# Integer softmax of an attention layer: row sums and three of eight value diagonals on GpSimd, one activation table set for logarithm and exponential

## The reference, cut to what matters

```python
x_int = x / scaling_factor
x_int = x_int - x_int.max(axis=-1, keepdims=True)
x0_int = jnp.floor(x0 / scaling_factor)
x_int = jnp.maximum(x_int, n * x0_int)
q = jnp.floor(x_int / x0_int)
r = x_int - x0_int * q
...
z = r * (r + b_int) + c_int
exp_int = jnp.maximum(jnp.floor(z * 2.0 ** (n - q)), 0.0)
exp_sum = exp_int.sum(axis=-1, keepdims=True)
ratio = jnp.round(exp_sum / jnp.maximum(exp_int, 1.0))
...
rounds = _log_round(ratio)
...
return jnp.where(mask, 0.0, 2.0 ** (-qlog))
```

## Time and profile before

| | |
|---|---|
| time, median of 3 runs | 598.61 us (598.5 to 599.84) |
| the profiled execution, span from first to last instruction | 604.2 us |
| busy in the span | PE 495.1, DVE 319.2, ACT 206.6, POOL 154.5 us |
| mean granted PE clock | 0.909 of full speed |
| part of the span that the change touches | about 139 to 187 us |

### The profile page before, as it was taken

How to read it: one execution, slowest core, us unless ns; L and a number is a source line. 1 busy time by engine, 2 the same in 40 slices (tenths; PEclk the granted TensorE clock), 3 DMA queues, 4 the chain that set the end, 5 groups by cost and what they waited for, 6 DMA issues and landing times.

```text
span 604.2 us, 12487 instructions
## 1 busy us (share of the span) xinstructions
PE 495.1 (82%) x4400; PEld 457.5 (76%) x4401; DVE 319.2 (53%) x1037; ACT 206.6 (34%) x441; POOL 154.5 (26%) x148
## 2 busy tenths in 40 slices
PE   4999999986443596799998399767999999999960
PEld 4999996575442485799997286756999999999950
DVE  1668999788999786122221356892222222222207
ACT  3630014868984164233334052260121112121110
POOL 1592000000001002465433000005444543443220
PEclk9999999999567686999999589879999999999995
DMA  8995000000009123587779900022666655667117
GB/s 314 408 335 160 15 1 1 1 3 1 0 2 312 30 105 118 168 210 192 162 234 322 295 4 0 1 106 59 190 190 192 201 164 164 190 182 211 34 49 291
DMA packets 40659, 84.86 MB, mean 140 GB/s; under 512 B 7270, under 2 KB 23186, under 8 KB 39586
## 3 DMA queue, kind: packets, MB, share of 16 engines
q1 hardware_dynamic: 33218, 72.81, 37.0%
q0 software_dynamic: 7392, 11.41, 8.3%
HBM read 70.33 MB, written 13.86 MB: 139 GB/s over the span
## 4 chain that ended last, share of the span: by engine, by line
PE 69%; DVE 16%; DMA 6%; ACT 4%; issue 2%; another core or an unknown queue 1%; POOL 0%; SPq 0%; DVEq 0%; ACTq 0%; POOLq 0%
PE ps L1137 18%; PE ps L887 14%; PE ps L1113 12%; PE ps L1121 6%; DMA made<-xT,to_i 3%; DVE h L1924 2%; PE ps L827 2%; PE ps L1002 1%; PE ps L974 1%; DVE xT L1771 1%; PE ps L975 1%; PE ps L1104 1%; PE ps L867 1%; PE ps L868 1%; PE ps L852 1%
## 5 line engine op out<-in xcount | busy, mean ns | idle before, releaser
L1137 PE MATMUL ps<-arena,xn 128*128 x696 | 123.1, 327 | 2.1 <-ACT xn L777 2.1
L1137 PEld LDWEIGHTS ps<-arena,xn 128*128 128x128 f32 x696 | 111.8, 190 | 4.2 <-issue 4.0
L515 POOL DMA_INDIRECT xT<-rows,from_i x58 | 56.3, 971 | 175.8 <-DVE from_i L1785 127.5
L530 POOL DMA_INDIRECT made<-xT,to_i x58 | 67.8, 1170 | 100.9 <-DVE xT L1823 65.9
L887 PE MATMUL ps<-arena 128*128 128x192 f32 (+1 forms) x588 | 85.6, 336 | 9.0 <-ACT arena L556 9.0
L887 PEld LDWEIGHTS ps<-arena 128*128 128x128 f32 (+1 forms) x588 | 83.9, 196 | 9.3 <-ACT arena L556 8.6
L1113 PE MATMUL ps<-xn,arena 128*128 128x128 f32 x696 | 87.2, 275 | 3.2 <-DVE xn L1813 3.2
L1113 PEld LDWEIGHTS ps<-xn,arena 128*128 128x128 f32 x696 | 84.9, 192 | 3.5 <-issue 3.5
L780 ACT ACTIVATE xn<-ps 128x384 f32<-128x384 f32 x78 | 32.6, 493 | 144.7 <-PE ps L1123 110.0
L1811 DVE COPY xn<-ps 128x128 f32<-128x128 f32 x58 | 16.9, 292 | 118.9 <-PE ps L1105 98.2
L777 ACT ACTIVATE xn<-ps,b_all 128x128 f32<-128x128 f32 x114 | 30.8, 389 | 63.5 <-PE ps L1123 51.9
(11 more groups left out here) (373 smaller groups left out, 765.6 us busy)
## 6 DMA issues: line engine op xcount, KB each, us to landing
arena<-ffn_a SPq DMA_DIRECT2D x58, 384.0 KB
arena<-ffn_b SPq DMA_DIRECT2D x116, 96.0 KB
arena<-x_blocks SPq DMA_DIRECT2D x16, 384.0 KB, 7.0
arena<-x_strips SPq DMA_DIRECT2D x3, 1536.0 KB, 12.2
arena<-ffn SPq DMA_DIRECT2D x4, 1152.0 KB
rows<-xn SPq DMA_DIRECT2D x8, 384.0 KB, 2.3
arena<-made SPq DMA_DIRECT2D x8, 384.0 KB, 6.6
arena<-tok_w SPq DMA_DIRECT2D x8, 288.0 KB, 7.3
```

The costliest lines, as they stand in the source:

```text
L515: pool.indirect_dma_start(sx[:, k % 6], None, F["src"], bass.IndirectOffsetOnAxis(from_i[:, k:k + 1], 0)).then_inc(sem(f"sx_in{k % 6}"), 16)
L530: pool.indirect_dma_start(F["made"], bass.IndirectOffsetOnAxis(to_i[:, k:k + 1], 0), yo[:, k % 3], None, compute_op=(ALU.add, ALU.bypass)[ ...
L1137: mm = pe.matmul(ps[:, result_bank(k, N), 0:DIM], hT[:, u % 2, 128 * c:128 * c + 128], F["w2"][:, bass.ds(e2 + DIM * c, DIM)], start=(c == ...
```

## The change

Four things are done in the softmax:

1. The row sums leave DVE. POOL makes them from `Ee` by adding 8 to 8, 4 to 4, 2 to 2 and 1 to 1 elements of each row, in a buffer `pairs` of its own, and DVE waits for them (`row_sums`) ahead of the last instruction of `ratios`.
2. Since POOL still reads `Ee` then, `ratios` begins in another buffer, `quot`, and comes back to `Ee` with its last instruction. `quot` lies where `wx` lies, so `weights(0)` waits for the second `ratio`.
3. POOL makes three of the eight diagonals: (0, part 0) and (1, part 0) ahead of the row sums, as soon as the first values and the masks are there, and (3, part 1) after them. ACT makes the other five, in another order.
4. ACT loads one table set, `natural_log_exp_and_others`, ahead of its wait for the scalars (L675), for both Ln and Exp.

Beside that, semaphores are merged: `tok_b_in` into `cst_in`, `b2_in` into `ffn_in0`, `ones_row`, `gate_set` and `wnat_set` into `pool_set`, `gate_logit` and `soft_in` into `exp_in`, and `gate_exp` and `soft_exp` into `exp_out`, with the counts that are waited for raised to match.

```diff
+        quot = view(18432, [3072])
...
-            sp.dma_start(tok_b_row[:], tok_b).then_inc(sem("tok_b_in"), 16)
+            sp.dma_start(tok_b_row[:], tok_b).then_inc(sem("cst_in"), 16)
...
-            sp.wait_ge(sem("cst_in"), 16)
+            sp.wait_ge(sem("cst_in"), 32)
...
-            sp.dma_start(b2_all, ffn0_b2.to_broadcast([128, E0 * DIM])).then_inc(sem("b2_in"), 16)
+            sp.dma_start(b2_all, ffn0_b2.to_broadcast([128, E0 * DIM])).then_inc(sem("ffn_in0"), 16)
...
+            def on_diagonal(j, part):
+
+                b = slice(96 * part, 96 * part + 96)
+                v_rows = v_sb.rearrange("p t (h d) -> p (t h) d", h=HEADS)
+                pool.tensor_scalar(vbd[:, b, j, :], v_rows[:, b], stat[:, 244 + j:245 + j], None,
+                                   ALU.mult).then_inc(sem("v_pool"), 1)
+
+            def row_sums(part):
+
+                pool.wait_ge(sem("exp_int"), part + 1)
+                E = Ee[:, 1536 * part:1536 * part + 1536].rearrange("p (a b) -> p a b", b=16)
+                pairs = view(24960, [96, 8])
+                link(pool.tensor_tensor(pairs, E[:, :, 0:8], E[:, :, 8:16], ALU.add))
+                for half in (4, 2):
+                    link(pool.tensor_tensor(pairs[:, :, 0:half], pairs[:, :, 0:half], pairs[:, :, half:2 * half], ALU.add))
+                pool.tensor_tensor(rsum[:, 96 * part:96 * part + 96], pairs[:, :, 0], pairs[:, :, 1], ALU.add
+                                   ).then_inc(sem("row_sums"), 1)
+
+            pool.wait_ge(sem("r_ready"), 1)
+            pool.wait_ge(sem("v_act"), 4)
+            on_diagonal(0, 0)
+            on_diagonal(1, 0)
+            row_sums(0)
+            pool.wait_ge(sem("row_sums"), 1)
+            row_sums(1)
+            pool.wait_ge(sem("v_act"), 8)
+            on_diagonal(3, 1)
             pool.wait_ge(sem("o_ps"), 4)
...
+            act.preload_act_table_set("natural_log_exp_and_others")
             act.wait_ge(sem("scalars"), 1)
...
             guess(1)
+            on_diagonal(2, 0)
             thirds(0)
-            on_diagonal(0, 0)
-            on_diagonal(1, 0)
-            on_diagonal(2, 0)
+            on_diagonal(3, 0)
+            on_diagonal(0, 1)
             thirds(1)
-            on_diagonal(3, 0)
-            for j in range(4):
-                on_diagonal(j, 1)
+            on_diagonal(1, 1)
+            on_diagonal(2, 1)
...
-                pe.wait_ge(sem("v_act"), 12 if tq < 2 else 16)
+                pe.wait_ge(sem("v_act"), 10 if tq < 2 else 13)
+                pe.wait_ge(sem("v_pool"), 2 if tq < 2 else 3)
...
             def exponentials(part):
-                c, b = part_of[part]
+                c = part_of[part][0]
                 dve.wait_ge(sem("power_ready"), 2 * part + 2)
                 dve.scalar_tensor_tensor(Ee[:, c], Ee[:, c], k_sq, half_ps[part], ALU.add, ALU.mult).then_inc(sem("exp_int"), 1)
-                dve.wait_ge(sem("exp_int"), part + 1)
-                link(dve.tensor_reduce(rsum[:, b], rows(Ee[:, c]), AX.X, ALU.add))
 
             def ratios(part):
 
-                R = Ee[:, part_of[part][0]]
+                E, R = Ee[:, part_of[part][0]], quot[:, part_of[part][0]]
                 dve.wait_ge(sem("guess"), part + 1)
-                link(dve.scalar_tensor_tensor(R, R, 2.0 ** -30, half_ps[part], ALU.mult, ALU.mult))
+                link(dve.scalar_tensor_tensor(R, E, 2.0 ** -30, half_ps[part], ALU.mult, ALU.mult))
                 link(dve.scalar_tensor_tensor(R, R, 2.0, half_ps[part], ALU.subtract, ALU.mult))
-                dve.scalar_tensor_tensor(rows(R.bitcast(I32)), rows(R), -2.0 ** -30, across(rsum, part), ALU.mult,
+                dve.wait_ge(sem("row_sums"), part + 1)
+                dve.scalar_tensor_tensor(rows(E.bitcast(I32)), rows(R), -2.0 ** -30, across(rsum, part), ALU.mult,
                                          ALU.mult).then_inc(sem("ratio"), 1)
...
+                if part == 0:
+                    dve.wait_ge(sem("ratio"), 2)
```

More of the change, by code:

```diff
@@ L479, in link @@
                 pool.wait_ge(sem("pool_step"), steps[0])
-            pool.memset(xT1[K1:128, :], 1.0).then_inc(sem("ones_row"), 1)
-            pool.wait_ge(sem("ones_row"), 1)
+            pool.memset(xT1[K1:128, :], 1.0).then_inc(sem("pool_set"), 1)
+            pool.wait_ge(sem("pool_set"), 1)
             link(pool.memset(wnat[96:128, 5:7, :], 0.0))
             for w in gate_w1:
-                pool.memset(w[K1:128], 0.0).then_inc(sem("gate_set"), 1)
-            pool.memset(wnat[64:128, 4, :], 0.0).then_inc(sem("wnat_set"), 1)
-            pool.wait_ge(sem("wnat_set"), 1)
+                pool.memset(w[K1:128], 0.0).then_inc(sem("pool_set"), 1)
+            pool.memset(wnat[64:128, 4, :], 0.0).then_inc(sem("pool_set"), 1)
+            pool.wait_ge(sem("pool_set"), 4)
             pool.wait_ge(sem("w_row"), 1)
@@ L505, in _ @@
                 pool.tensor_tensor(s[:, 0, :], s[:, 0, :], s[:, 2, :], ALU.add).then_inc(sem("w_sums"), 1)
+            def on_diagonal(j, part):
[21 more added lines that the diff above has]
+            on_diagonal(3, 1)
             pool.wait_ge(sem("o_ps"), 4)
-            pool.memset(aqT1[K1:K1 + 3], 1.0).then_inc(sem("ones_row"), 1)
+            pool.memset(aqT1[K1:K1 + 3], 1.0).then_inc(sem("pool_set"), 1)
             def exchange(F):
@@ L810, in _ @@
             ins.then_inc(sem("lin_a"), 1)
-            act.wait_ge(sem("gate_logit"), 1)
-            act.activation(stat[:, 501:502], stat[:, 500:501], ACT.Exp, scale=-1.0).then_inc(sem("gate_exp"), 1)
+            act.wait_ge(sem("exp_in"), 1)
+            act.activation(stat[:, 501:502], stat[:, 500:501], ACT.Exp, scale=-1.0).then_inc(sem("exp_out"), 1)
             transposed(3)
-            act.wait_ge(sem("soft_in"), 1)
+            act.wait_ge(sem("exp_in"), 2)
             d16 = rt[:, 432:448]
-            act.activation(d16, d16, ACT.Exp).then_inc(sem("soft_exp"), 1)
+            act.activation(d16, d16, ACT.Exp).then_inc(sem("exp_out"), 1)
             all_norms(1)
@@ L860, in logits @@
                 if i == 0:
-                    pe.wait_ge(sem("gate_set"), 2)
+                    pe.wait_ge(sem("pool_set"), 3)
                 pe.wait_ge(sem("xT0_ready"), 4 * (1 + 2 * n) + i + 1)
@@ L929, in _ @@
                     if (name, b) == ("m2", 1):
-                        pe.wait_ge(sem("cst_in"), 16)
+                        pe.wait_ge(sem("cst_in"), 32)
                         pe.wait_ge(sem("w_sums"), 2)
-                        pe.wait_ge(sem("tok_b_in"), 16)
                         pe.matmul(ps[:, 4, 0:DIM], ones, sum_g[:, 0, :], start=True, stop=True)
@@ L954, in _ @@
             pe.wait_ge(sem("bias_in"), 16 * BIASES)
-            pe.wait_ge(sem("ones_row"), 1)
+            pe.wait_ge(sem("pool_set"), 1)
             def qk_free(n):
@@ L1062, in _ @@
             pe.wait_ge(sem("aq_act"), 5)
-            pe.wait_ge(sem("ones_row"), 2)
+            pe.wait_ge(sem("pool_set"), 5)
             pe.wait_ge(sem("wp_ready"), 2)
@@ L1173, in experts @@
                 up(1, 1, 0)
-                pe.wait_ge(sem(f"ffn_in{n}"), 16 if n == 0 else 16 * E1 // 2)
+                pe.wait_ge(sem(f"ffn_in{n}"), 32 if n == 0 else 16 * E1 // 2)
                 pe.wait_ge(sem(f"tiles_ready{n}"), 1)
@@ L1348, in _ @@
             dve.wait_ge(sem("blk_read"), 16)
-            dve.wait_ge(sem("cst_in"), 16)
+            dve.wait_ge(sem("cst_in"), 32)
             away, away_sq = stat[:, 100:101], stat[:, 101:102]
@@ L1464, in _ @@
             token_row(1)
-            dve.wait_ge(sem("wnat_set"), 1)
+            dve.wait_ge(sem("pool_set"), 4)
             dve.wait_ge(sem("wnat_in"), 128)
@@ L1736, in route @@
                     link(dve.tensor_tensor(d16, c16, a16, ALU.subtract))
-                    dve.tensor_tensor(d16, d16, stat[:, 464:480], ALU.mult).then_inc(sem("soft_in"), 1)
+                    dve.tensor_tensor(d16, d16, stat[:, 464:480], ALU.mult).then_inc(sem("exp_in"), 1)
                 dve.wait_ge(sem("rank_ps"), n + 1)
@@ L1799, in route @@
                 if n:
-                    dve.wait_ge(sem("soft_exp"), 1)
+                    dve.wait_ge(sem("exp_out"), 2)
                     link(dve.tensor_scalar(c16, d16, 1.0, None, ALU.add))
@@ L1832, in copies @@
                 if n == 0:
-                    dve.wait_ge(sem("b2_in"), 16)
+                    dve.wait_ge(sem("ffn_in0"), 32)
                 dve.wait_ge(sem(f"tiles_ready{n}"), 1)
@@ L1893, in _ @@
             link(dve.tensor_tensor(ltmp[:, 0:16], ps[:, 6, 0:16], cst[:, C_SEL:C_SEL + 16], ALU.mult))
-            dve.tensor_reduce(stat[:, 500:501], ltmp[:, 0:16], AX.X, ALU.add).then_inc(sem("gate_logit"), 1)
+            dve.tensor_reduce(stat[:, 500:501], ltmp[:, 0:16], AX.X, ALU.add).then_inc(sem("exp_in"), 1)
             plus_normed(12, 16)
-            dve.wait_ge(sem("gate_exp"), 1)
+            dve.wait_ge(sem("exp_out"), 1)
```

## The result

The changed kernel took a median of 604.17 us (20 runs, 599.86 to 605.83), the kernel before 598.83 us beside it (20 runs). The ratio of the two is 1.0072 [1.0051, 1.0094], which is 4.3 us slower, where 0.7 slower was forecast and 602.0 was the upper end.

What follows compares the result with a forecast made beforehand. The prediction took DVE and ACT as tied in the softmax, then DVE alone setting the end. Its terms, -2.5 + 2.8 + 0.4 = +0.7 us on 598.61, gave 599.3 us, range 595.8 to 602.0.

Steps and rivals of the forecast that it cites:

- The gain, -2.5: Softmax: without its row sums on DVE and table loads between Ln and Exp on ACT, ratios end 2.5 us earlier.
- One table load: ACT: one load of 1.28 us ahead of the wait for the scalars replaces four, fitting idle time but for 0.1.
- The two diagonals hold DVE, "2 x 1.4 = 2.8": Quotients of part 0: POOL's first two diagonals, 1.5 us each, hold DVE 1.4 us each, 2.8 us on the chain.
- `row_sums(1)` meets L1609, 0.4: Ratios of part 0: POOL's sums for part 1 meet DVE's two-input L1609, and DVE loses 0.4 us.
- The third diagonal "is over before L1609 of part 1": POOL's diagonal after the sums runs 163.1 to 164.6, ending before L1609 of part 1, so costs nothing.
- Nothing for L1599, L1607 and L1608: DVE's instructions with only one SBUF input lose nothing beside POOL's sums; if held, up to 4.0 us a part.
- Row sums in 4.0 us a part: POOL makes one part's row sums in 4.0 us, with 2.5 and 3.8 us to spare before DVE asks.
- The same clock, and nothing outside the softmax: PE idles before its products as long as before, so same clock; no difference expected outside 139 to 187 us.
- the slow multiplication: Rival, chance 0.12: POOL's diagonals take 3.44 us each, two hold DVE 6.7 us; +5.5, 604.1 us.
- DVE is not held: Rival, chance 0.37: no contention in quotients, 596.1 us (0.27), or POOL is the one that waits, 597.1 us (0.10).
- late sums: Rival, chance 0.08: POOL's sums take 8 us a part, DVE stalls 4.2 us in ratios; +1.7 without holds, +4.5 with.
- loads that stay: Rival, chance 0.03: each ACT function still loads its table set; 0 without holds, about +3 us with them.

Runs made afterwards that it cites:

- e1_sums_table: Changed kernel with all eight diagonals back on ACT; row sums on POOL and one table set stay: 595.53 us, ratio 0.9942 to the kernel before.
- the probe: e1_sums_table with five POOL instructions of 1344 elements added between the experts layers, a DVE instruction beside each; one execution profiled, not timed against the kernel before.
- e6_later: Kernel before with one table set and diagonals 0 and 1 of part 0 on POOL, begun after quotients: 599.94 us, ratio 1.0016.
- e4_sums: e1_sums_table without the one table set, so row sums on POOL and four table loads as before: 599.03 us, ratio 0.9995 to the kernel before.
- e5_third: e1_sums_table with diagonal 3 of part 1 on POOL after the row sums: 596.55 us, ratio 0.9969 to the kernel before.

## Why the prediction was wrong

The mechanisms were named rightly, and one size was far off. The sum was -2.5 + 2.8 + 0.4 = +0.7. Measured in the stretch it is -2.50 + 6.69 + 0.62 = +4.81 (the 0.62 is 0.20 for the sums and 0.42 for the third diagonal), and the stretch is 4.82 longer.

- **The gain, -2.5: right.** -2.30 in `e1_sums_table`, and -2.50 without the 0.20 of the meeting with L1630, which the prediction booked apart. That the two covers were tied is shown from both sides: taking away one alone moves the stretch by 0.23 or less.
- **One table load: right.** One row of 1.28 us at 139.80 and none between Ln and Exp; it delayed nothing on DVE, as the two L708 ran from 141.09 to 144.31, the first of them for half of that, and DVE's quotients, which need the first, began only at 143.95 behind DVE's own work. That one set serves both functions is what the Trainium skill has (ScalarE: Activation LUTs, "Table sets: the hidden batching unit"), and these rows agree.
- **The two diagonals hold DVE, "2 x 1.4 = 2.8": the step that failed, by its price.** "It reads one tensor, so I take 1.5." The term was put at 2.8 us and measured 6.69. A diagonal takes 4.15 us undisturbed. It even lies above the bound of 3.44, which was the rate of POOL's addition: I took one input to be cheaper than two at most, and the rows show a multiplication at 2.6 ns an element over an addition at 2.1. The hold itself came where it was put, on the second and third instruction of `quotients(0)`, and for the reason given. Of its size, L1620 had 3.99 us of the first diagonal before it when it began and lost 3.80; L1622 had 3.98 of the second and lost 2.89, since it was let in some 0.9 us before that one's end (1.82 - 0.15 - 0.73, as in the probe).
- **`row_sums(1)` meets L1609, 0.4: right in place.** It cost 0.20, and POOL bore most of it: its pair of L522 took 2.98 in place of the 1.58 of part 0. L1636 began at 167.50, 0.35 us before the end of the first of the pair, and the second then stood until L1636 was over (1.90 us, where it takes 0.51 undisturbed).
- **The third diagonal "is over before L1609 of part 1": wrong, for the same price.** It ran from 170.25 to 174.40, L1636 began at 172.95, so 1.45 us before its end, and lost 0.42: it too was let in early and ended 0.73 after POOL, as L1622 did.
- **Nothing for L1599, L1607 and L1608: right.** Their counterparts L1627, L1633 and L1634 took 1.77, 1.75 and 1.75 beside POOL's running sums, and L1610 and L1612 of `e6_later` kept theirs beside diagonals.
- **Row sums in 4.0 us a part: right.** 161.02 to 164.91 is 3.9 for part 0; part 1's took 5.3 with the hold above. No instruction of `ratios` waited for them.
- **The same clock, and nothing outside the softmax: right as far as the runs tell.** The granted clock of PE was 0.50 while it idled ahead of its products, and 0.68 from 187 to 240 us, in both executions. The 4.82 us of the stretch lie inside the interval of the timed ratio, so no cost outside it is needed; one of a microsecond could hide in that interval. The merged semaphores weren't tried alone.

Of the rivals, the slow multiplication (604.1 us, "it decides from about 2.0 us a diagonal on") is what happened. Its sum came nearer than its parts: it had 3.44 us a diagonal, held for nearly the whole, which is 6.7, where 4.15 us with an early entry make 6.69. That these two agree is luck. For the third diagonal it had 0.9, measured 0.42. It had a chance of 0.12, because I chose between bounds far apart by the copy's row: the copy is no nearer to a multiplication for having one input. With nothing but these two rows the middle, 2.45 us, would already have lain on the slow side of that point. "DVE is not held" is refuted by L1620 and L1622, late sums and loads that stay by the rows of `row_sums` and of ACT above.

The Trainium skill (SBUF — State Buffer, "Who interferes with whom") has the second instruction to start blocked for the whole of the other. This case's traces agree for L1620 (0.62 to 4.42) and beside POOL's addition (1.56 to 3.61). For a two-input instruction of DVE beside POOL's multiplication they agree in part, since it was let in some 0.55 to 0.9 us early. By that rule L1622 would have lost some 3.8 as L1620 did, and the two together 7.6 us (an estimate), not 6.69.

Not settled: why a multiplication on POOL is dearer than an addition, why DVE's two-input instructions are let in early beside the one and not beside the other, and whether moving diagonals to POOL late in `e1_sums_table` would gain. ACT's diagonals are not on its chain in this stretch, so I expect nothing, and it wasn't tried.

## What to carry to other kernels

Price an operation on an engine by a row of that very operation. If the trace has none, take no other operation's rate for an upper bound: here GpSimd's multiplication was dearer than the copy by far and dearer than the addition of two tensors, and a forecast that turns on such a price should be as wide as that says. Before work goes to an idle GpSimd, list what DVE runs beside it: in these runs an instruction with two SBUF inputs or of a fast one-tensor kind was held, one with an input in PSUM or a reduction was not, and a later start can make the same work free (`e6_later`). Where two engines are tied, relieve both or neither: each half alone gave nothing, both gave 2.3 us, and the version with just those two, `e1_sums_table`, stands at 0.9942 of before where the whole change stands at 1.0072.

## What the runs showed of the hardware beyond that

- GpSimd's multiplication of 1344 f32 by a scalar took 3.60 us, longer than the addition of a tensor of that size to itself (2.43) and 2.8 times the copy (1.30). A column in place of the constant cost 0.09 us (3.69), spread output in place of packed none (3.60 both, with the constant).
- A DVE instruction of 128x4 elements, 0.17 us by itself, took 3.29 us beside such a multiplication. The hold went by the kind of the instruction, not by its size.
- It works both ways. When DVE's L1630 of `e1_sums_table` lay beside POOL's pair of halving additions, the pair took 2.98 us, against 1.58 in `e4_sums`, where DVE was in no such instruction, and DVE lost 0.20.
- Where DVE's two-input instruction was let in early, its end lay at one distance from POOL's: 0.73 us for 1536 elements (L1622 and L1636 of the change, L1634 of `e5_third`), 0.86 for 1344 (twice in the probe), wherever in POOL's multiplication it had begun.
